# Holding one pass of table writes at TensorE's steps, as the loop around it does

## The chip, the cores and the metric

The kernel runs on one core of a Trainium2 chip. The metric is the device time of one execution in microseconds, lower being better. The kernel before takes 1842.63 us, the median of three runs (1838.82 to 1842.83).

## The reference

Two transformer layers over 32 batches (`B`) of 256 tokens with 256 features. The first layer is cross attention with relu instead of softmax, followed by a feed-forward network with weights of plus and minus one. The second is a cross attention with one memory row per query picked by argmax, and then a mixture of 64 experts, of which each token uses 8, with 128 places for each expert. Cut to what matters here:

```python
x = x + tanh(g_xattn[0]) * L0_xattn(layernorm(x), ctx, ctx)
x = x + tanh(g_ffn[0])   * L0_ffn(layernorm(x))
x = x + tanh(g_xattn[1]) * L1_xattn(layernorm(x), ctx)
h = layernorm(x).reshape(-1, H)                 # 8192 tokens
shared = silu(gu[:, :Is]) * gu[:, Is:] @ shared_down_w * sigmoid(h @ shared_gate_w)
w, idx = top_k(softmax(h @ gate_w), 8)
pos = running count of tokens per expert        # over all tokens, in order
buf[e_flat, min(pos, 128)] = h[tok]             # rows handed to the experts
y = sum over 8 of out_e[e_flat, slot] * w       # 0 where pos >= 128
x = x + tanh(g_ffn[1]) * (y + shared)
```

## The kernel before

Each engine has its own program, written out by hand; the engines meet only through semaphores. The work on a batch is cut into four stages, and the stages of four batches overlap: in pass `n`, TensorE computes the feed-forward network of batch `n` (`b_l0`, `b_l1`, `b_l2`), the first attention of batch `n+1`, the second attention and the shared expert of batch `n-1` (`c_...`, `d_gu`), and the end of batch `n-2` (`d_dn`, `d_cp`). The hand-written sequences `first(n)` and `second(n)` set TensorE's order.

Passes -1 to 2 stand outside a hardware loop, passes 3 to 30 are the loop (`Fori(3, NB - 1)`, with `NB` 32), and pass 31 stands outside again. Then come `first(32)` and `last_batch(31)`, called the drain below, and the 64 experts.

For every batch, GpSimd (POOL) writes 128 token rows at a time to a table in memory, sorted by expert: `scatter(b, group)`, an indirect DMA at L637 that moves 128 rows of 321 numbers. A batch needs 16 of these, cut in eleven groups `a` to `k` (2, 1, 1, 2, 1, 1, 1, 1, 2, 2 and 2 writes). POOL's pass `n` issues groups `g` to `k` of batch `n-3` and `a` to `f` of batch `n-2`, between its other duties. These are `take_ctx` (a copy), `take_keys` (operands of the next attention logits), `keep_x1` (a copy at L648), and `ln_coef`, the inverse root of the layer norms at L653, for which VectorE (DVE), then ScalarE (ACT) and then TensorE wait.

In the loop, seven of the eleven groups (`a`, `b`, `f`, `g`, `h`, `j`, `k`) are held: POOL waits for a step of TensorE and then runs a tiny filler operation (`plain`, L579, pool_pad) before it issues the write. The steps are the transposition of the attention's output (`tr_rdy[4]`, L1240) for `a` and `b`, the third part of the shared expert (`gu_rdy`, L1031) for `f`, the first two pairs of `b_l0` (`l0_rdy`, L1117) for `g` and `h`, the first attention logits (`lg_rdy`, L1193) for `j`, and the first transposition of the probabilities (`pt_rdy`, L1208) for `k`. In the code outside the loop the condition `not isinstance(b, int)` leaves all this out, and a group goes out as soon as POOL comes to it.

The order of POOL's pass 31 is: `g` and `h` of batch 28, `take_ctx`, `i`, `j`, `k` of batch 28, `take_keys`, `a` and `b` of batch 29, `keep_x1`, `ln_coef(3, 30)`, `c` and `d`, `ln_coef(2, 31)`, `e` and `f`. Behind the pass follow `g` to `k` of batch 29 and the batches 30 and 31. On SyncE, `pass_rows(29)` (L418) overwrites the rows in SBUF after the 16 writes of batch 28 have landed, and loads of expert weights are queued behind it.

Of the kernel before, what the change touches and what calls it, by code (L numbers as in the profile page):

```python
# [18 lines left out]
NB, S, D = 32, 256, 256  # L19
# [74 lines left out]
def build(nc, x, ctxT, maskT, g_xattn, g_ffn, wq0, wk0, wv0, bq0, bk0, bv0, k0, k1, k2, s0, s1, s2,  # L94
          wqT1, wkvT1, wcT1, gates_w, sgu_w, sdown_w, e_wts, out, table):
    es = ExitStack()
    with es:
# [249 lines left out]
        def written(b):  # L347

            return (xs_z, slot_z) if isinstance(b, int) and b == NB - 1 else (xs, slot)
# [177 lines left out]
        def _(pool):  # L527
# [49 lines left out]
            def plain(site):  # L577

                return g.tensor_tensor(pool_pad[:, site:site + 1], pad_in[:, :], pad_in[:, :], ALU.mult)  # L579
# [41 lines left out]
            def scatter(b, group):  # L621
                if group == "a":
                    pool.wait_ge(slots_ok, b + 1)
                    pool.wait_ge(tok_ok, b + 1)
                    pool.wait_ge(xr_out, 16 * b + 16)
                paced = {"a": (tr_rdy[4], b + 2), "b": (tr_rdy[4], b + 2), "f": (gu_rdy.sem, gu_rdy.nth(2, b + 1)), "g": (l0_rdy.sem, l0_rdy.nth(0, b + 3)),
                         "h": (l0_rdy.sem, l0_rdy.nth(1, b + 3)), "j": (lg_rdy.sem, lg_rdy.nth(0, b + 2)),
                         "k": (pt_rdy.sem, pt_rdy.nth(0, b + 2))}
                if not isinstance(b, int):
                    if group in paced:  # L630
                        pool.wait_ge(*paced[group])
                    if group in paced:
                        plain(8 + "abcdefghijk".index(group))
                rows, slots = written(b)
                for i in GROUPS[group]:
                    t, k = divmod(i, TOPK)
                    g.indirect_dma_start(  # L637
                        out=table, out_offset=bass.IndirectOffsetOnAxis(ap=slots[:, t, k:k + 1], axis=0),
                        in_=rows[:, t, :], in_offset=None, bounds_check=NT - 1, oob_is_err=False,
                    ).then_inc(scattered, 16)  # L640
# [40 lines left out]
            def body(n):  # L681
                m, c, d, e = n + 1, n - 1, n - 2, n - 3
                if on(e):
                    scatter(e, 'g')
                    scatter(e, 'h')
                if on(n):
                    take_ctx(n)
                if on(e):
                    scatter(e, 'i')
                    scatter(e, 'j')  # L690
# [1337 lines left out]
```

## Time and profile before

| what | value |
| --- | --- |
| median of three runs | 1842.63 us |
| lowest and highest run | 1838.82, 1842.83 us |
| profiled execution | 1847.19 us |
| its span, first to last instruction | 1845.2 us |
| PE, DVE, POOL, ACT busy | 91%, 72%, 55%, 52% of the span |
| one pass of the loop | 47.4 us |
| pass 31, outside the loop | 57.3 us |
| the drain, to the first expert | 83 us |
| TensorE's mean granted clock | 0.969 |

The profile is one execution on the chip. PE is TensorE. A pass is bounded here by the start of the last part of `d_gu` in two successive passes. A row of a timeline gives start and duration of an instruction, and in brackets how long its engine had been idle before it and what ended that; "issue" and "remote" mean that nothing the profile shows ended it. In the table, pass 31 does the same work as a pass of the loop less the first stage of a next batch.

### The profile page before, as it was taken

Reading aid. Unit: us, or ns where it says so; the run is one execution under the profiler, and the core shown is the slowest. Engines: PE = TensorE matmul, PEld = TensorE weight load, DVE = VectorE, ACT = ScalarE, POOL = GpSimd, SP = SyncE. Lnnn points to the kernel's source line nnn. Section 1 sums busy time; section 2 is a strip of 40 time slices with the busy share of each in tenths; the row PEclk is TensorE's granted clock in tenths of the full one; section 3 lists DMA queues with packets and bytes.
Section 4 is the critical chain, followed back from the end, with each engine's and each line's share of the span. In section 5 each row is a group of like instructions: output and inputs, shape, how many; then the busy total and the mean of one; then the engine's idle time right before and its main releaser. Section 6 shows DMA issues by size and latency. Waiting matters only on the chain.

```text
span 1845.2 us, 51326 instructions
## 1 busy us (share of the span) xinstructions
PE 1681.7 (91%) x17188; PEld 1418.1 (77%) x17188; DVE 1330.1 (72%) x4610; ACT 964.5 (52%) x2789; POOL 1023.1 (55%) x1627
## 2 busy tenths in 40 slices
PE   5799999999999999999999999999999998458785
PEld 4588888888788888878888888888888876347775
DVE  5477777777677777777777787777777865436554
ACT  3455555555555555555555555555555544214443
POOL 4125666666566666655666666666666653345555
PEclk9899999999999999999999999999999998579999
DMA  7411111111111111101111111111010012138886
GB/s 235 141 17 48 50 46 44 47 51 39 30 30 28 37 26 43 29 21 30 33 30 26 33 26 26 26 27 26 25 30 21 21 57 74 48 96 215 197 198 136
DMA packets 134336, 108.98 MB, mean 59 GB/s; under 512 B 70559, under 2 KB 123753, under 8 KB 134296
## 3 DMA queue, kind: packets, MB, share of 16 engines
q1 hardware_dynamic: 100504, 89.30, 16.7%
q0 software_dynamic: 33792, 19.17, 5.9%
q8 instruction: 22, 0.36, 0.1%
q14 instruction: 18, 0.15, 0.0%
HBM read 51.63 MB, written 111.84 MB: 89 GB/s over the span
## 4 chain that ended last, share of the span: by engine, by line
PE 69%; DMA 8%; DVE 7%; issue 6%; ACT 4%; another core or an unknown queue 4%; POOL 2%; SPq 0%; POOLq 0%; DVEq 0%; ACTq 0%
PE bank L1133 22%; PE bank L1031 8%; DMA out<-ey,aid 6%; PE bank L1117 6%; PE ps_yo L1031 4%; PE ps_m L1031 4%; PE ps_lg L1193 4%; PE ps_lg L1031 3%; PE ps_yo L1149 3%; PE ps_tr L1057 3%; PE ps_m L1231 2%; PE ps_pt L1031 2%; PE ps_pt L1208 2%; ACT xr L774 2%
## 5 line engine op out<-in xcount | busy, mean ns | idle before, releaser
L637 POOL DMA_INDIRECT table<-xs,slot x496 | 505.4, 1019 | 199.3 <-issue 171.8
L1133 PE MATMUL bank<-h_h,held 128*128 128x256 f16 x2048 | 267.6, 274 | 2.8 <-DVE h_l L1616 1.7
L1133 PE MATMUL bank<-h_l,held 128*128 128x256 f16 x2048 | 266.9, 273 | 0.7 <-issue 0.7
L579 POOL TENSOR_TENSOR pool_pad<-pad_in 128x1 f32<-128x1 f32 x382 | 75.0, 196 | 325.4 <-PE ps_tr L1240 163.8
L838 ACT ACTIVATE p<-ps_lg,rmax 128x77 f32<-128x77 f32 x1024 | 235.5, 351 | 7.3 <-DVE rmax L1681 7.0
L1133 PEld LDWEIGHTS bank<-h_l,held 128*128 128x128 f16 x2048 | 201.2, 98 | 25.0 <-issue 1.1
L1133 PEld LDWEIGHTS bank<-h_h,held 128*128 128x128 f16 x2048 | 193.7, 98 | 25.4 <-issue 3.3
L1616 DVE SCALAR_TENSOR_TENSOR h_l<-bank,h_h 128x512 f16<-128x512 f32 x256 | 175.0, 684 | 27.8 <-ACT h_h L824 22.4
L653 POOL TENSOR_TENSOR rs<-nt,minushalf 128x2 f32<-128x2 f32 x128 | 92.5, 722 | 163.5 <-DVE nt L1578 152.4
L844 ACT ACTIVATE pt_h<-ps_pt 128x384 f16<-128x384 f32 x128 | 62.8, 491 | 189.0 <-PE ps_pt L1208 189.0
L741 POOL DMA_INDIRECT out<-ey,aid x64 | 98.7, 1542 | 97.1 <-DVE aid L1963 57.4
L1681 DVE TENSOR_REDUCE rmax<-ps_lg 128x8 f32<-128x616 f32 x128 | 102.1, 797 | 54.6 <-PE ps_lg L1193 52.1
L824 ACT ACTIVATE h_h<-bank 128x512 f16<-128x512 f32 x128 | 76.6, 598 | 119.1 <-PE bank L1133 119.1
L819 ACT ACTIVATE h_h<-bank 128x512 f16<-128x512 f32 x128 | 76.4, 597 | 92.4 <-PE bank L1117 92.4
L1149 PE MATMUL ps_yo<-held,h_h 128*128 128x256 f16 x512 | 118.2, 276 | 0.1
L1149 PE MATMUL ps_yo<-held,h_l 128*128 128x256 f16 x512 | 118.0, 273 | 0.0
L1117 PE MATMUL bank<-xt_h,held 128*128 128x256 f16 x512 | 99.5, 277 | 8.3 <-DVE dn_l L1510 5.9
L1565 DVE BATCH_NORM_STATS2 stats<-x 128x6 f32<-128x256 f32 x256 | 96.0, 417 | 13.4 <-DMA x<-in_x 3.7
L1031 PE MATMUL bank<-xt_h,gu_h 128*128 128x256 f16 x512 | 99.3, 276 | 0.8 <-DVE ac L1770 0.6
L1031 PE MATMUL bank<-xt_l,gu_h 128*128 128x256 f16 x512 | 99.4, 276 | 0.0
L1117 PE MATMUL bank<-xt_l,held 128*128 128x256 f16 x512 | 99.3, 276 | 0.0
L1031 PE MATMUL bank<-xt_h,gu_l 128*128 128x256 f16 x512 | 99.2, 276 | 0.0
(279 smaller groups left out, 4574.9 us busy)
## 6 DMA issues: line engine op xcount, KB each, us to landing
ew<-in_e_wts SPq DMA_DIRECT2D x48, 384.0 KB
table<-xg SPq DMA_DIRECT2D x8, 1284.0 KB, 15.9
xg<-table SPq DMA_DIRECT2D x64, 160.5 KB
xs<-xr SPq DMA_DIRECT2D x31, 320.0 KB, 2.7
x<-in_x SPq DMA_DIRECT2D x32, 256.0 KB
out<-x SPq DMA_DIRECT2D x32, 256.0 KB
table<-xs,slot POOLq DMA_INDIRECT x496
held<-in_e_wts SPq DMA_DIRECT2D x16, 384.0 KB, 4.4
```

What stands on the lines that cost most here:

```text
L637: g.indirect_dma_start(out=table, out_offset=bass.IndirectOffsetOnAxis(ap=slots[:, t, k:k + 1], axis=0), in_=rows[:, t, :], in_offset=None ...
L653: g.tensor_tensor(rs[i][:, :], nt[i][:, 0, :], minushalf[:, :], ALU.pow).then_inc(ln_root[i], 1)
L741: g.indirect_dma_start(out=out, out_offset=bass.IndirectOffsetOnAxis(ap=aid[u][:, 0:1], axis=0), in_=ey[u][:, :], in_offset=None, bounds_c ...
L824: a.activation(h1_h[:, 2 * j:2 * j + 2, :], two(bank[j % 2]), ACT.Relu).then_inc(l1_hi.sem, 1)
L838: ins = a.activation(p32[:, h * S2:(h + 1) * S2], ps_lg[:, h // HB, h % HB * S2:(h % HB + 1) * S2], ACT.Exp, bias=rmax[r % 2][:, h:h + 1])
L1031: ins = mm(out_, s_, m_, start=(start and i == 0), stop=(stop and i == len(seq) - 1))
L1117: ins = mm(two(bank[j % 2])[:, m % 2, :], s_, m_, start=(k == 0), stop=(k == 3))
L1133: ins = mm(two(bank[j % 2])[:, m % 2, :], wb1[:, k, m * P:(m + 1) * P], hp[:, k, :], start=(i == 0 and k == 0), stop=(i == 1 and k == FK - 1))
L1149: ins = mm(two(ps_yo)[:, t, :], hp[:, k, t * P:(t + 1) * P], wb2[:, k, :], start=(i == 0 and k == 0), stop=(i == 1 and k == FK - 1))
L1565: last = v.bn_stats(stats[i][:, t, :], src[:, t, :])
L1616: v.scalar_tensor_tensor(hl[:, 2 * j:2 * j + 2, :], two(bank[j % 2]), 0.0, hh[:, 2 * j:2 * j + 2, :], ALU.max, ALU.subtract).then_inc(lo.s ...
L1681: v.tensor_reduce(rmax[r % 2][:, :].rearrange("p (g h) -> p g h", g=2), lg, AX, ALU.max, negate=True).then_inc(z_ok.sem, 1)
```

## The change

One condition in `scatter` is widened. Batch 28 (`NB - 4`, groups `g` to `k`) and groups `a` to `f` of batch 29 (`NB - 3`) are now held too, wherever they stand outside the loop, which is pass 31. The waits and the fillers are those of the loop, seven of each.

```diff
@@ scatter(b, group) @@
-                if not isinstance(b, int):
+                if not isinstance(b, int) or b == NB - 4 or b == NB - 3 and group in "abcdef":
                     if group in paced:
                         pool.wait_ge(*paced[group])
                     if group in paced:
                         plain(8 + "abcdefghijk".index(group))
```

No other engine's program changes, nor does POOL's before pass 31. POOL's first row after the loop's branch was two writes (`g`, `h`); each now has its wait for `l0_rdy` ahead of it.

POOL in the middle of pass 31, behind `take_ctx` and up to the filler of `take_keys`. The rows L637 are table writes (groups `i`, `j`, `k` of batch 28), the rows L579 fillers with the semaphores they wait for:

```order
-L637 DMA table<-xs,slot 8192x321 x6
+L637 DMA table<-xs,slot 8192x321 x2
+L579 TENSOR_TENSOR pool_pad<-pad_in 128x1 [waits lg_rdy]
+L637 DMA table<-xs,slot 8192x321 x2
+L579 TENSOR_TENSOR pool_pad<-pad_in 128x1 [waits pt_rdy]
+L637 DMA table<-xs,slot 8192x321 x2
 L579 TENSOR_TENSOR pool_pad<-pad_in 128x1 [waits lg_rdy,vc_ok,vp_ev,kp_ev]
```

Six writes in a row became three pairs, of which the second waits for the logits and the third for the transposed probabilities of batch 30.

POOL behind `take_keys` in the same pass. The writes are groups `a` and `b` of batch 29, L648 is the copy of `keep_x1`, L653 the root of `ln_coef(3, 30)`:

```order
-L637 DMA table<-xs,slot 8192x321 [waits xr_out,tok_ok,slots_ok]
-L637 DMA table<-xs,slot 8192x321 x2
+L579 TENSOR_TENSOR pool_pad<-pad_in 128x1 [waits xr_out,tr_rdy4,tok_ok,slots_ok]
+L637 DMA table<-xs,slot 8192x321 x2
+L579 TENSOR_TENSOR pool_pad<-pad_in 128x1 [waits tr_rdy4]
+L637 DMA table<-xs,slot 8192x321
 L648 COPY x_kept<-x 128x512 [waits x2_ok,x1_ok]
 L653 TENSOR_TENSOR rs<-nt,minushalf 128x2 [waits ln_st3]
```

The three writes, and so the copy and the root behind them, now wait for the transposed attention output of batch 30.

POOL at the end of the pass, where `e` and `f` of batch 29 are followed at once by its `g` to `k`:

```order
 L653 TENSOR_TENSOR rs<-nt,minushalf 128x2 [waits ln_st2]
-L637 DMA table<-xs,slot 8192x321 x10
+L637 DMA table<-xs,slot 8192x321
+L579 TENSOR_TENSOR pool_pad<-pad_in 128x1 [waits gu_rdy]
+L637 DMA table<-xs,slot 8192x321 x9
```

Nine of the ten writes now stand behind a wait for the third part of the shared expert.

## Rows read from the trace of the kernel before

**Rows 1.** The first line of the page.

```profile
span 1845.2 us, 51326 instructions
```

**Rows 2.** Stretches: span; PE, PEld, DVE, ACT, POOL busy; clock; DMA share, GB/s.

```profile
1457.20:1504.70 47.50, 45.37 (x492) 37.98 (x489) 35.88 (x126) 25.41 (x77) 28.05 (x49) 1.00 0.18 55
1504.70:1562.00 57.30, 49.47 (x477) 39.16 (x477) 34.83 (x116) 24.98 (x74) 23.28 (x32) 0.91 0.18 60
```

**Rows 3.** Line L848 on ACT in the whole trace: count, durations, what ended its idle.

```profile
L848 ACT ACTIVATE vb<-ps_tr x32: 511/511/512, 80.8 to 1575.7; 128x408 f16<-128x408 f32 x32
...
  PE ps_tr L1215: 67.9, 31
  remote: 6.9, 1
```

**Rows 4.** Timelines of ACT, DVE and PE in pass 31: start, duration, instruction.

```profile
1521.26 0.51 ACT L848 ACTIVATE vb<-ps_tr 128x408 f16<-128x408 f32 x1 [6.92 <-remote]
...
1518.37 0.80 DVE L1681 TENSOR_REDUCE rmax<-ps_lg 128x8 f32<-128x616 f32 x1 [2.04 <-remote]
...
1515.72 0.47 PE L1215 MATMUL ps_tr<-vc,wide 77*128 77x34 f16 x12
...
1518.34 0.60 PE L1133 MATMUL bank<-h_h,held 128*128 128x256 f16 x4 [0.29 <-issue]
...
1521.20 0.93 PE L1133 MATMUL bank<-h_l,held 128*128 128x256 f16 x7 [0.45 <-issue]
```

**Rows 5.** Timeline of POOL, from the last loop pass into the drain.

```profile
1488.12 0.20 POOL L579 TENSOR_TENSOR pool_pad<-pad_in 128x1 f32<-128x1 f32 x1 [5.79 <-PE ps_tr L1240]
...
1500.29 1.04 POOL L637 DMA_INDIRECT table<-xs,slot  x1 [2.75 <-issue]
...
1511.68 0.19 POOL L579 TENSOR_TENSOR pool_pad<-pad_in 128x1 f32<-128x1 f32 x1 [3.06 <-PE ps_tr L1031]
...
1512.54 1.01 POOL L637 DMA_INDIRECT table<-xs,slot  x1 [0.16 <-issue]
...
1518.99 0.98 POOL L637 DMA_INDIRECT table<-xs,slot  x1 [0.30 <-issue]
1535.93 0.19 POOL L579 TENSOR_TENSOR pool_pad<-pad_in 128x1 f32<-128x1 f32 x1 [15.96 <-PE ps_lg L1193]
...
1544.10 0.63 POOL L648 COPY x_kept<-x 128x512 f32<-128x512 f32 x1
1550.21 0.72 POOL L653 TENSOR_TENSOR rs<-nt,minushalf 128x2 f32<-128x2 f32 x1 [5.49 <-DVE nt L1578]
...
1569.62 0.97 POOL L637 DMA_INDIRECT table<-xs,slot  x1 [0.30 <-issue]
1594.54 0.97 POOL L637 DMA_INDIRECT table<-xs,slot  x1 [23.95 <-DVE slot L1761]
```

**Rows 6.** Timeline of PE, the steps for which the held groups would wait.

```profile
1515.49 0.29 PE L1193 MATMUL ps_lg<-kb_h,qp_l 64*128 64x308 f16 x2
...
1525.17 0.90 PE L1208 MATMUL ps_pt<-ident,p 128*128 128x128 f32 x3
...
1542.57 0.76 PE L1240 MATMUL ps_tr<-ident,att 128*128 128x128 f32 x4 [0.72 <-DVE att L1694]
...
1558.75 0.38 PE L1031 MATMUL bank<-xt_h,gu_l 128*128 128x256 f16 x2
```

**Rows 7.** Stretches in which TensorE was granted half of its clock.

```profile
1522.50:1529.30 6.80, 5.27 (x28) 3.63 (x29) 4.74 (x20) 4.50 (x18) 0.00 (x0) 0.50 0.15 52
1542.90:1546.30 3.40, 3.40 (x18) 2.44 (x17) 1.29 (x2) 1.08 (x2) 1.59 (x2) 0.51 0.04 5
```

**Rows 8.** Timelines of DVE and SyncE: who waits for the copy; a late step; the row copy.

```profile
1554.65 0.75 DVE L1630 SCALAR_TENSOR_TENSOR x<-ps_yo,sc,x_kept 128x512 f32<-128x512 f32 x1 [0.54 <-PE ps_yo L1149]
...
1569.34 0.24 DVE L1643 MAX8 am<-ps_tr 128x8 f32<-128x77 f32 x1 [4.04 <-issue]
...
1527.82 0.60 SPq L418 DMA_DIRECT2D xs<-xr  x1
```

## The prediction, made before the changed kernel ran

> **What bounds the kernel now.** I read the stretches first, since the change touches one pass of 32. The last pass of the loop takes 47.50 us, and pass 31 takes 57.30 us for no more work [rows 2]: DVE, ACT and POOL are all less busy in it, and TensorE's granted clock is 0.91 instead of 1.00. So pass 31 holds 9.8 us over a pass of the loop, and that is all the change can get at, in a span of 1845.2 us [rows 1]. About 1.9 us of it comes from before the change's reach: POOL issued group `d` of batch 29 after an idle of 2.75 us with no cause in the profile [rows 5], still inside the loop's last pass, and the last part of `d_gu` behind it is that much late. This leaves 7.9 us.
>
> Next I looked at where those 7.9 us arise, by engine. ACT's copy at L848 waits for TensorE's L1215. In 31 of its 32 executions its idle ended with that step (67.9 us in all, 2.2 us each); once it was 6.92 us with nothing to end it [rows 3]. That once is pass 31: L1215 was over at 1515.72 + 0.47 = 1516.19, and ACT began at 1521.26 [rows 4], 5.1 us late. All softmax steps of batch 30 are queued behind it on ACT. In the same microseconds DVE had an idle of 2.04 us without a cause, ended at 1518.37, and TensorE, in a run of matmuls that wait for nobody, went in pieces from 1518.34 to 1521.20 [rows 4]. Three engines halt together, and the one thing that goes on is POOL's table writes: six, from 1512.54 to 1518.99 + 0.98 = 1519.97, one each 1.29 us [rows 5]. The passes 1 and 2 stand outside the loop as well, and their L848 is among the 31 without a halt. So straight-line code alone doesn't make it; straight-line code together with a dense stream of writes is what this place has to itself. A second such halt stands in the drain: DVE's L1643 with 4.04 us of idle without a cause at 1569.34 [rows 8], again inside a stream, whose last write starts at 1569.62 [rows 5].
>
> After the halt the clock goes down: TensorE has half of it (1.2 of 2.4 GHz) from 1522.5 to 1529.3 and from 1542.9 to 1546.3 [rows 7]. These two stretches hold 5.27 and 3.40 us of PE work, which at the upper level would be half of that, so up to 2.6 + 1.7 = 4.3 us hang on it.
>
> **The change part by part.** Seven fillers of 0.2 us and their waits on POOL: 1.4 us of work, and an estimated 0.9 us from the end of the step waited for to the write. POOL has 15.96 us of idle before `take_keys` and 5.49 us before the root at 1550.21 [rows 5], so nothing of that is paid as such. What matters is when each piece comes out.
>
> `g` and `h`: their steps, two pairs of the first layer, lie before the step of TensorE on which the filler at 1511.68 waits [rows 5]. They go out before it, and `take_ctx` and `i` (1512.54) stay where they are. Cost nothing.
>
> `j`: its step, the logits, ends at 1515.49 + 0.29 = 1515.78 [rows 6]. The writes come at about 1516.6 and 1517.9, 1.5 us later than before (third and fourth place in the stream, 1515.1 and 1516.4).
>
> `k`: its step begins at 1525.17 [rows 6] and comes from ACT's softmax, behind the halt. The two writes leave the stream (they were at 1517.7 and 1518.99) and come at about 1526.9 and 1528.2. POOL is done by 1529.2, 6.7 us before `take_keys` at 1535.93, less what that step comes earlier. SyncE's copy of the rows, at 1527.82 now [rows 8], must wait for their landing and comes about 2.5 us later, as do the weight loads queued behind it on SyncE. Nobody on this pass waits for them before `a` does, and `a` is held past that. Cost nothing.
>
> So instead of six writes between 1512.5 and 1520.0 there are four, and the last is out at 1518.9. What does the halt give back? From below: ACT began 1.29 us after the last write was out; with the last write 1.1 us earlier it begins 1.1 us earlier. From above inside this reading: the halt goes with the number of writes, and 5.1 us times 2/6 is 1.7 us. I take 1.5 us. The clock stays low in the same stretches, since three and a half microseconds of halt remain.
>
> `a` and `b`: the step ends at 1542.57 + 0.76 = 1543.33 [rows 6]. Writes from 1544.2, three of them with a second filler until about 1548.3, then the copy, which ends at about 1549.0 instead of 1544.73. DVE wants the copy at 1554.65 [rows 8], 5.6 us later. The root behind it started at 1550.21, on DVE's word [rows 5]: slack 1.2 us. Cost nothing while that holds.
>
> `f`: the third part of the shared expert ends near 1559.1 (its last matmuls start at 1558.75 [rows 6]), the write comes 0.8 us later than before, and so do the nine behind it. The stream ends at 1571.4 instead of 1570.6. POOL's next write had to wait until 1594.54 anyway [rows 5]. But the DVE halt at 1569.34 lies in this stream and could stretch with it: 0 to 0.8 us. I take 0, since it ended before the stream did.
>
> Sum: -1.5 + 0 = -1.5 us, with ends -0.3 (1.1 given back, 0.8 paid) and -1.7. The profiled execution would take 1847.19 - 1.5 = 1845.7 us. It lies 4.6 us over the median of the three runs, so I carry the difference over to the median: 1842.63 - 1.5 = 1841.1, say 1841 us.
>
> The Trainium skill bears on why the engines halt. Its page Runtime: NRT & Kernel Launch, section Instruction fetch mechanics, says that an engine's code is fetched by DMA in blocks while the block before runs, and that this is mostly hidden. By that page alone, thinning out the writes would give 0 us; the halt of 5.1 us [rows 4] is not hidden here. Its page DMA: Bandwidth & Descriptors, section Queues, rings and completion order, says that a DMA engine takes turns between queues packet by packet, by which a fetch would be slowed by every write in flight. No row read here shows a fetch waiting.
>
> **The rivals.** *The halt goes away whole.* With never more than two writes back to back, as in the passes of the loop, the three engines may never halt. For it speaks that 31 of 32 executions of L848 have none [rows 3]; against it, that `i` and `j` still put four writes in 6.4 us where the halt begins. It gives back 5.1 us, and up to 4.3 us of clock [rows 7], but no more than the 7.9 us left over: 1842.6 - 7.9 = 1834.7 us.
>
> *The halt has nothing to do with the writes.* All engines leave the loop here within some microseconds, and the halt may belong to that. DVE's and ACT's halts both start within 12 us of the pass's beginning at 1504.7; POOL's idle of 2.75 us [rows 5] came with no stream at all, which speaks for this. Then POOL's writes move in idle time and the time is 1842.6 us.
>
> *Slower: the hold uses up POOL's cover ahead of the root.* Before, POOL sat idle for 5.49 us ahead of the root at 1550.21. Now it has 1.2 us. If POOL has a halt of its own between 1543 and 1550, the root of `ln_coef(3, 30)` is late, and DVE, ACT and TensorE's next transposition with it, on the path. It decides from 1.2 us on. A halt of POOL's known size, 2.75 us, costs 1.5 us; one of ACT's 5.1 us costs 3.9, and with the clock held down as in the second stretch [rows 7] 5.6 us. Its middle is +3: 1845.6 us. POOL's code has grown by seven fillers and their waits, so that a halt may fall elsewhere than before.
>
> **How the numbers follow.** The forecast has 0.36, the whole halt gone 0.26, no connection 0.24, slower 0.14. The lower end of the range is 1834, just under the first rival; the upper is 1845, which leaves out about half of the slower case and, below, some of the first rival where the runs scatter down by their 4 us: together under 0.2. A measurement of this kernel can tell about 0.3%, 5.5 us, from no change. Only the first rival goes past it downward: 0.26. Upward goes the far end of the slower case, and a little for what I have not thought of: 0.06. The rest, 0.68, is within.
>
> **What would show it.** In the changed trace, pass 31 between the same two steps takes 55.8 us by the forecast, 49.4 if the halt is gone, 57.3 without a connection. ACT's L848 has its one long idle shortened to about 5.4 us by the forecast, to 2.2 if the halt is gone. `k` is issued after the first transposition at L1208, the copy L648 comes at about 5 us after the filler for L1240, and the root after it must still be ended by DVE's nt; if it starts straight after the copy, the slower case holds. The half-clock stretch after 1522 stays in the forecast and goes in the first rival. The forecast is wrong if the halt keeps its length while the last write moves forward, or if a halt of the same kind turns up at a place that had none, on POOL above all.

## The result, and the profile after

The changed kernel took 1835.42 us (median of 13 runs, 1830.50 to 1837.67), the kernel before on the same chip 1841.92 us (13 runs, 1838.75 to 1847.60). The ratio is 0.9958, with a 95% interval of [0.9947, 0.9968], so 0.4% faster; between the medians lie 6.5 us. The time lies in the range of the prediction and near its first rival, not near the forecast of 1841. As will be seen, the figure holds for one sort of chip only. The ratios here and below are taken over all runs of both kernels and needn't equal the ratio of the two medians.

The profiled execution of the changed kernel took 1833.93 us. Its page begins, against [rows 1]:

```profile
span 1832.2 us, 51334 instructions
```

Eight instructions more: seven fillers, and one wait that has an instruction of its own. The two stretches that answer to [rows 2] (span; PE, PEld, DVE, ACT, POOL busy; clock; DMA share; GB/s):

```profile
1454.58:1502.00 47.42, 45.25 (x491) 37.84 (x489) 35.88 (x126) 25.40 (x76) 28.05 (x48) 1.00 0.19 55
1502.00:1551.35 49.35, 45.72 (x471) 37.63 (x472) 34.89 (x116) 24.97 (x74) 23.96 (x38) 0.97 0.21 70
```

The last pass of the loop is as it was. Pass 31 went from 57.30 to 49.35 us, so 7.95 us came back, and the clock in it rose from 0.91 to 0.97. Of the 13.0 us between the two spans, another 2.7 us arose before pass 31 begins (1502.0 for 1504.7), where the change does nothing; a second profile of the changed kernel, below, doesn't have them. 3.0 us came from the drain and 0.65 us went back in the experts. One execution against one can be off by some microseconds: the profiled one of the kernel before took 1847.19 us, 5.3 us over the median of its 13 runs, and the medians say 6.5. There is no second profile of the kernel before, on either sort of chip.

ACT's L848, against [rows 3], over the whole trace:

```profile
L848 ACT ACTIVATE vb<-ps_tr x32: 511/511/511, 81.4 to 1563.3; 128x408 f16<-128x408 f32 x32
...
  PE ps_tr L1215: 68.1, 32
```

All 32 now end their idle with TensorE's step; the long one with "remote" is gone. The timelines of the place, against [rows 4] and [rows 6], first ACT, then DVE, then PE:

```profile
1512.83 0.51 ACT L848 ACTIVATE vb<-ps_tr 128x408 f16<-128x408 f32 x1 [1.88 <-PE ps_tr L1215]
...
1513.04 0.80 DVE L1681 TENSOR_REDUCE rmax<-ps_lg 128x8 f32<-128x616 f32 x1
...
1512.33 0.47 PE L1215 MATMUL ps_tr<-vc,wide 77*128 77x34 f16 x12
1512.78 1.03 PE L1133 MATMUL bank<-h_h,held 128*128 128x256 f16 x8
...
1516.37 0.31 PE L1193 MATMUL ps_lg<-mrow,row 64*128 64x308 bf16 x2
...
1516.99 0.55 PE L1208 MATMUL ps_pt<-ident,p 128*128 128x128 f32 x3
```

From L1215 to L848's start there were 5.54 us before (1515.72 to 1521.26) and there are 0.50 now (1512.33 to 1512.83). DVE doesn't wait at L1681, and TensorE's matmuls at L1133 stand in whole groups of eight. L1208 comes 4.66 us after L1215, where it came 9.45 us after it, and runs at the full clock (0.55 us instead of 0.90).

POOL, against [rows 5]:

```profile
1509.53 1.01 POOL L637 DMA_INDIRECT table<-xs,slot  x1 [0.16 <-issue]
...
1512.57 0.19 POOL L579 TENSOR_TENSOR pool_pad<-pad_in 128x1 f32<-128x1 f32 x1 [0.74 <-PE ps_lg L1193]
...
1514.61 0.98 POOL L637 DMA_INDIRECT table<-xs,slot  x1 [0.30 <-issue]
1517.63 0.19 POOL L579 TENSOR_TENSOR pool_pad<-pad_in 128x1 f32<-128x1 f32 x1 [2.04 <-PE ps_pt L1208]
1518.35 1.00 POOL L637 DMA_INDIRECT table<-xs,slot  x1 [0.53 <-issue]
...
1533.21 0.20 POOL L579 TENSOR_TENSOR pool_pad<-pad_in 128x1 f32<-128x1 f32 x1 [5.08 <-PE ps_tr L1240]
...
1537.67 0.63 POOL L648 COPY x_kept<-x 128x512 f32<-128x512 f32 x1
1540.05 0.72 POOL L653 TENSOR_TENSOR rs<-nt,minushalf 128x2 f32<-128x2 f32 x1 [1.75 <-DVE nt L1578]
...
1549.03 0.18 POOL L579 TENSOR_TENSOR pool_pad<-pad_in 128x1 f32<-128x1 f32 x1 [0.39 <-PE bank L1031]
...
1560.30 0.99 POOL L637 DMA_INDIRECT table<-xs,slot  x1 [0.30 <-issue]
```

`i` and `j` are four writes between 1509.53 and 1515.59, `k` stands alone behind L1208, the root is still ended by DVE. The last write of the stream behind `f` starts at 1560.30. DVE in that stream, against [rows 8]:

```profile
1555.62 0.24 DVE L1643 MAX8 am<-ps_tr 128x8 f32<-128x77 f32 x1 [1.11 <-issue]
...
1561.42 0.48 DVE L1659 TENSOR_SCALAR mrow<-ps_tr 128x308 bf16<-128x308 f32 x1 [3.98 <-remote]
```

The idle ahead of L1643 shrank from 4.04 to 1.11 us, and one of 3.98 us turned up further on, ahead of L1659, where the kernel before had 1.24 us, ended by TensorE's L1176. For [rows 7], the same places of pass 31 (17.8 and 38.2 us after its start) hold no lowered clock:

```profile
1519.80:1526.60 6.80, 6.80 (x93) 5.41 (x91) 4.62 (x11) 3.90 (x16) 1.60 (x5) 1.00 0.53 176
1540.20:1543.60 3.40, 3.09 (x25) 2.12 (x24) 1.11 (x3) 1.69 (x3) 2.60 (x3) 1.00 0.01 0
```

One stretch of 3.4 us at half the clock remains in the pass, from 1533.5 to 1536.9.

**What a halt is.** "remote" and "issue" say only that the profile found no one to blame, since TensorE's row had long ended. The trace also records when each semaphore was written, and that settles who was waited for. In the kernel before, the semaphore that L1215 raises was written at 1521.24, 5.06 us after the end of the row (1516.19 by the profile); ACT's row starts 0.02 us later. The one that L1193 raises was written at 1518.35, 2.56 us late, and DVE's L1681 starts at 1518.37. So the waiting engines weren't halted at all: they waited for TensorE's completions, and those were late. TensorE's own rows go with it: in the pieces of [rows 4] they start again at 1518.34 and at 1521.20, within 0.04 us of the two writes. From the same records, for the steps whose reader began right then:

| step of TensorE | written after the row's end, before | with the change |
|---|---|---|
| L1193, pass 31 | 2.56 us | 0.02 us |
| L1215, pass 31 | 5.06 us | 0.01 us |
| L1031 (`qp`), drain | 3.68 us | 0.74 us |
| L1176, drain | 0.77 us | 3.62 us |
| L1031 (`gw`), drain | 2.58 us | 1.84 us |
| L1031 (`ps_yo`, read by L1780), drain | 2.71 us | 0.41 us |
| L1231, median of the first of each loop pass | 1.70 us | 1.72 us |
| most others in the loop, median | 0.01 us | 0.01 us |

The Trainium skill, Perfetto Trace Analysis, section Per-instruction lifecycle: what the profiler-reported window actually captures, says that TensorE's end time is an estimate from the size of the instruction, while its semaphore is pushed when PSUM has acknowledged the bytes. The trace agrees that the row's end is no measurement: the two are 0.01 us apart as a rule and 5.06 us apart once. It doesn't show what happened in the 5.06 us.

### The profile page after: what moved, and what is told of

It reads as the page before. It is cut to its first block, busy times and chain, and to the rows that moved or that the text cites. A ratio compares the mean times of both kernels' runs of the same rounds, so it can differ in the third digit from the quotient of the medians.

```text
span 1832.2 us, 51334 instructions
## 1 busy us (share of the span) xinstructions
PE 1670.9 (91%) x17188; PEld 1413.6 (77%) x17188; DVE 1331.1 (73%) x4610; ACT 964.8 (53%) x2789; POOL 1027.4 (56%) x1634
## 4 chain that ended last, share of the span: by engine, by line
PE 68%; DMA 8%; DVE 7%; issue 6%; ACT 4%; another core or an unknown queue 4%; POOL 3%; SPq 0%; POOLq 0%; DVEq 0%; ACTq 0%
PE bank L1133 22%; PE bank L1031 8%; DMA out<-ey,aid 6%; PE bank L1117 6%; PE ps_yo L1031 4%; PE ps_m L1031 4%; PE ps_lg L1193 4%; PE ps_lg L1031 3%; PE ps_yo L1149 3%; PE ps_tr L1057 2%; PE ps_m L1231 2%; POOL table L637 2%; PE ps_pt L1031 2%; PE ps_pt L1208 2%
## 5 line engine op out<-in xcount | busy, mean ns | idle before, releaser
L637 POOL DMA_INDIRECT table<-xs,slot x496 | 507.4, 1023 | 194.1 <-issue 192.8
L1133 PE MATMUL bank<-h_h,held 128*128 128x256 f16 x2048 | 265.8, 273 | 1.7 <-DVE h_l L1616 1.7
L1133 PE MATMUL bank<-h_l,held 128*128 128x256 f16 x2048 | 266.3, 273 | 0.0
L579 POOL TENSOR_TENSOR pool_pad<-pad_in 128x1 f32<-128x1 f32 x389 | 75.9, 195 | 320.2 <-PE ps_tr L1240 169.1
L1133 PEld LDWEIGHTS bank<-h_l,held 128*128 128x128 f16 x2048 | 200.8, 98 | 23.6
L1133 PEld LDWEIGHTS bank<-h_h,held 128*128 128x128 f16 x2048 | 192.9, 98 | 23.4 <-issue 1.8
L653 POOL TENSOR_TENSOR rs<-nt,minushalf 128x2 f32<-128x2 f32 x128 | 93.0, 727 | 157.2 <-DVE nt L1578 145.3
L1681 DVE TENSOR_REDUCE rmax<-ps_lg 128x8 f32<-128x616 f32 x128 | 102.1, 798 | 48.3 <-PE ps_lg L1193 47.8
L1031 PE MATMUL bank<-xt_h,gu_h 128*128 128x256 f16 x512 | 98.4, 274 | 1.7 <-DVE ac L1770 1.6
L1031 PE MATMUL bank<-xt_h,gu_l 128*128 128x256 f16 x512 | 98.5, 274 | 0.0
L1031 PE MATMUL bank<-xt_l,gu_h 128*128 128x256 f16 x512 | 98.4, 274 | 0.0
```

What stands on the lines that cost most here:

```text
L637: g.indirect_dma_start(out=table, out_offset=bass.IndirectOffsetOnAxis(ap=slots[:, t, k:k + 1], axis=0), in_=rows[:, t, :], in_offset=None ...
L653: g.tensor_tensor(rs[i][:, :], nt[i][:, 0, :], minushalf[:, :], ALU.pow).then_inc(ln_root[i], 1)
L1031: ins = mm(out_, s_, m_, start=(start and i == 0), stop=(stop and i == len(seq) - 1))
L1133: ins = mm(two(bank[j % 2])[:, m % 2, :], wb1[:, k, m * P:(m + 1) * P], hp[:, k, :], start=(i == 0 and k == 0), stop=(i == 1 and k == FK - 1))
L1681: v.tensor_reduce(rmax[r % 2][:, :].rearrange("p (g h) -> p g h", g=2), lg, AX, ALU.max, negate=True).then_inc(z_ok.sem, 1)
```

## The experiments

The chips on which runs were made fall in two sorts, which I call A and B. The kernel before took 1841.92 and 1839.72 us in the two sessions on sort A (whether on one chip or two isn't recorded), and 1790.56, 1790.88, 1791.27 and 1794.37 us on sort B, three chips, one of them used twice. Which chip a run lands on can't be chosen. Of the kernels with an edit only the changed one came to both sorts; all those with a part of the change met sort B. That limits what follows.

**The change once more.** No edit; the kernel of the result.

> The change itself, measured again. In the four runs before this one the kernel before took 1790.6 us instead of 1841.9, ACT's L848 had no long idle even where the six writes stood in one stream, and DVE's first L1692 of a pass had lost the idle of 2.1 us without a cause that it has in 29 of 32 passes of the first traces. Theory D (the halts belong to the chip or to where the program lies on it): if the kernel before takes about 1790 us here too, the ratio is 0.999 to 1.002; if it takes about 1842 us, the ratio is 0.995 to 0.997. Theory A alone (dense writes halt the engines everywhere) would have given 0.996 in either case, and is already against the four runs.

On a chip of sort A: 1833.67 us (1830.60 to 1836.94) against 1839.72 us, ratio 0.9973, [0.9959, 0.9987]. Its stretch from L1215 of pass 31 to L1215 of the drain, and DVE in the drain:

```profile
1515.12:1566.79 51.67, 41.01 (x427) 33.05 (x426) 30.44 (x110) 20.45 (x64) 25.38 (x34) 0.96 0.20 66
...
1565.42 0.48 DVE L1659 TENSOR_SCALAR mrow<-ps_tr 128x308 bf16<-128x308 f32 x1 [5.33 <-remote]
```

The same stretch in the trace of the kernel before, and in the first trace of the changed one:

```profile
1515.72:1575.15 59.43, 45.90 (x427) 35.05 (x426) 30.78 (x111) 20.50 (x64) 23.63 (x29) 0.87 0.17 57
```

```profile
1512.33:1562.76 50.43, 41.10 (x427) 33.15 (x426) 30.70 (x109) 20.56 (x64) 25.37 (x34) 0.97 0.20 68
```

So 7.8 us come back in this stretch in the second profile and 9.0 in the first. In the second it begins at 1515.12, where the kernel before had 1515.72: the 2.7 us ahead of pass 31 were not the change's. The late completion at L1215 is gone in both profiles, the one ahead of L1659 is new in both.

**The change a third time.** No edit.

> The changed kernel once more. So far the kernel before took 1840 to 1842 us on two chips and 1790 to 1791 us on two others; the change was timed only on the former (ratios 0.9958 and 0.9973). Theory A: the gain is the halt of pass 31, and the halt exists only where a loop pass takes 47.4 us and TensorE's completions come late. Then here: if the kernel before takes about 1840 us, the ratio is again 0.995 to 0.998; if it takes about 1791 us, the ratio is 0.999 to 1.002, with pass 31 as long with the change as without. Rival B: the order of the writes has a worth of its own (TensorE's order suits the work behind it). Then the ratio is 0.996 to 0.998 on either kind of chip.

On a chip of sort B: 1797.43 us (1789.82 to 1799.32) against 1794.37 us (1790.85 to 1797.89), ratio 1.0013, [0.9998, 1.0027]. The stretches from L1215 to L1215, of pass 30 and of pass 31:

```profile
1427.24:1475.50 48.26, 46.69 (x507) 39.43 (x506) 38.14 (x130) 27.05 (x80) 28.97 (x49) 1.00 0.18 55
1475.50:1521.92 46.42, 40.96 (x428) 33.09 (x426) 30.87 (x111) 20.52 (x64) 23.38 (x32) 0.96 0.22 73
```

Theory A gets its number (0.999 to 1.002), rival B doesn't (0.996 to 0.998): the order of the writes has no such worth of its own there. In these runs the change gave something only where completions are late. The kernel before has no profile on sort B; the trace of "batch 29 alone" below, which leaves batch 28 as it was, takes 46.11 us between the same two steps (1477.08 to 1523.19), so 46.42 is not shorter.

**Half of the change at a time.** Batch 28 alone, batch 29 alone, and fillers without waits:

```
-                if not isinstance(b, int):
+                if not isinstance(b, int) or b == NB - 4:                          # batch 28 alone
+                if not isinstance(b, int) or b == NB - 3 and group in "abcdef":    # batch 29 alone
```

```
-                if not isinstance(b, int):
-                    if group in paced:
-                        pool.wait_ge(*paced[group])
+                if not isinstance(b, int) and group in paced:
+                    pool.wait_ge(*paced[group])
+                if not isinstance(b, int) or b == NB - 4 or b == NB - 3 and group in "abcdef":
```

> Only batch 28 is held (g, h, j, k), that is the writes up to take_keys; a, b and f of batch 29 go as before. Theory A: the whole gain in pass 31, ratio about 0.996 to 0.9965, L848 without a long idle. Theory C (the gain comes from the later copy and root behind a and b): none of it, ratio 1.0.

> Only a, b and f of batch 29 are held; the six writes of batch 28 stand in one stream as before. Theory A: L848 keeps its long idle, ratio 0.999 to 1.001. Theory C: the gain of the change, 0.996.

> The seven fillers stand in pass 31 as in the change, but none of the waits. POOL's code is as long as in the change and the writes go out as early as before, 0.2 to 0.5 us further apart. Theory A (the engines halt because table writes stream densely while they run code that is executed once): the six writes behind take_ctx still stand in one stream, ACT's copy L848 keeps its one long idle of about 7 us, and the time is that of before within 0.2% (0.998 to 1.002). Theory B (the gain comes from POOL's code being longer, which moves where a halt falls): the gain of the change, ratio about 0.996, L848 without the long idle.

All on one chip of sort B, where the kernel before took 1790.56 us (35 runs): batch 28 alone 1792.96 us, ratio 1.0017, [1.0008, 1.0026]; batch 29 alone 1791.00 us, 1.0003, [0.9994, 1.0013]; fillers alone 1791.61 us, 1.0008, [0.9997, 1.0019]. Fillers alone again on a second chip of that sort:

> Fillers without waits again, since the first four runs fell on a chip without the halts (kernel before 1790.6 us). Told by the kernel before in the same call. At about 1840 us: theory A (dense writes and code that is executed once, together) expects ACT's L848 with its long idle of about 7 us and a ratio of 0.999 to 1.001; theory B (POOL's code is longer, and a halt falls elsewhere) 0.996 to 0.998 and no long idle. At about 1790 us: ratio 1.000 and no long idle by both.

1791.50 us against 1790.88, ratio 1.0007, [0.9994, 1.0020]. None of them tells which half gives the gain, because there was no halt to remove; that there was none is what they show. "Batch 29 alone" leaves batch 28 as in the kernel before, with its six writes in a row while TensorE is at L1193 and L1215; POOL and ACT's L848 in its trace:

```profile
1473.90 1.01 POOL L637 DMA_INDIRECT table<-xs,slot  x1 [0.16 <-issue]
...
1480.36 0.98 POOL L637 DMA_INDIRECT table<-xs,slot  x1 [0.30 <-issue]
...
L848 ACT ACTIVATE vb<-ps_tr x32: 510/510/511, 80.5 to 1523.7; 128x408 f16<-128x408 f32 x32
...
  PE ps_tr L1215: 64.1, 32
```

Six writes from 1473.90 to 1481.34, L1215 at 1477.09 in the middle of them, and ACT waits at L848 as in any other pass. On sort B, then, the stream by itself delays no completion; on sort A no run tested it alone.

**Only `j` and `k`.** The two groups that fill the second half of that stream are held, nothing else.

```
-                if not isinstance(b, int):
+                if not isinstance(b, int) or b == NB - 4 and group in "jk":
```

> Only j and k of batch 28 are held, g and h go as early as before. Theory A in its narrow form (what counts is the stream of six behind take_ctx): the gain of the change, 0.996, L848 without a long idle. If g and h matter too (eight writes in 14 us instead of six in 7.5), part of the idle stays: 0.997 to 0.999.

> Only j and k of batch 28 held, again. With the kernel before at about 1840 us theory A expects the gain of the change, 0.996 to 0.998, and no long idle ahead of L848; if the hold of g and h is what counts, the idle of about 7 us stays and the ratio is 1.000. At about 1790 us: ratio 1.000.

> Only j and k of batch 28 held. Two calls gave a kernel before of 1790.6 and 1790.9 us without any halt, one call and the first measurement about 1840 us with halts. If this one has the kernel before at about 1840 us: theory A (the stream of six writes behind take_ctx meets code that is executed once) expects the gain of the change, 0.996 to 0.998, and no long idle ahead of ACT's L848; if g and h or a, b and f matter, the idle of about 7 us stays or the ratio is 0.999 to 1.001. At about 1790 us: 1.000 to 1.002.

> Only groups j and k of the pass of batch 28 wait for their steps; all else is as before. Theory A (what ends the halt is that the two writes of k leave the stream of six): where the kernel before takes about 1840 us, pass 31 loses its late completion at L1215 and the ratio is 0.995 to 0.998; where it takes about 1791 us, 1.000 to 1.002, as the earlier three. Rival C (the gain comes from the hold of a, b and f in batch 29, or from nothing in the order but from the place of the code): 0.999 to 1.001 where the kernel before takes about 1840 us, with the step at L1215 still about 5 us late.

Sort B each time: 1791.29 us, ratio 1.0007 [0.9997, 1.0018]; 1794.44 us, 1.0014 [0.9998, 1.0029]; 1795.87 us, 1.0009 [0.9990, 1.0029]; 1796.88 us, 1.0010 [0.9996, 1.0024]. For the cause of the halt they are inconclusive. For sort B they say something: these four, batch 28 alone (1.0017) and the whole change (1.0013) all lie about 0.1% above one, 1 to 3 us by the ratios. Only one interval leaves one out, and the fillers without waits, at 1.0008 and 1.0007, lie there as well, so this can't be put down to the waits. I found no stretch that holds the difference: the time from L1215 of the drain to the end of the span goes from 262 to 273 us among the profiles of sort B, more than what is looked for.

**The stream of six, moved.** `i`, `j` and `k` of batch 28 stay six writes in a row, but the row is held until the first L1208, behind the place of the halt.

```
-                if not isinstance(b, int):
-                    if group in paced:
-                        pool.wait_ge(*paced[group])
-                    if group in paced:
-                        plain(8 + "abcdefghijk".index(group))
+                if not isinstance(b, int) and group in paced:
+                    pool.wait_ge(*paced[group])
+                    plain(8 + "abcdefghijk".index(group))
+                elif isinstance(b, int) and b == NB - 4 and group == "i":
+                    pool.wait_ge(*paced["k"]); plain(18)
```

> The six writes of i, j, k stay one stream, but the stream starts only after TensorE's first L1208, some 5 to 10 us later than before. One filler, no other hold. With the kernel before at about 1840 us: if what counts is where the stream stands against the moment at which ACT, DVE and PE cross into code not yet read (about 11 us after the pass begins), L848 has no long idle and the ratio is 0.996 to 0.998; if a dense stream halts whoever runs, a halt of 3 to 5 us turns up at another step, at L1681, L844 or L838, and the ratio is 0.999 to 1.001. At about 1790 us: ratio 1.000, no halt.

> The six writes of i, j and k of batch 28 stay one stream, but the stream is held until TensorE's first L1208; a, b and f of batch 29 are not held. Theory A1 (a stream of six writes makes whichever completion of TensorE falls behind it come late): where the kernel before takes about 1840 us, the halt moves behind the first L1208 and stays some 5 us, ratio 0.999 to 1.001. Rival A2 (the halt hangs on writes at that one place, before L1215 of the pass, not on the number): the halt goes, ratio 0.995 to 0.998. Where the kernel before takes about 1791 us both say 1.000, as the earlier run.

Sort B again: 1791.25 us against 1790.88, ratio 0.9999 [0.9987, 1.0012], and 1793.39 us against 1794.37, ratio 0.9992 [0.9981, 1.0004]. POOL in the second:

```profile
1484.90 0.19 POOL L579 TENSOR_TENSOR pool_pad<-pad_in 128x1 f32<-128x1 f32 x1 [8.50 <-PE ps_pt L1208]
1485.64 1.02 POOL L637 DMA_INDIRECT table<-xs,slot  x1 [0.54 <-issue]
...
1492.08 0.97 POOL L637 DMA_INDIRECT table<-xs,slot  x1 [0.30 <-issue]
```

No late completion behind it either. Whether on sort A the halt would have followed the stream (A1) or stayed away (A2) stays open.

The pair also measures what the lowered clock costs. The same kernel, from L1215 of pass 31 to L1215 of the drain, once with and once without such a stretch, on two chips of sort B:

```profile
1476.97:1523.19 46.22, 40.68 (x428) 33.19 (x426) 30.63 (x111) 20.44 (x64) 25.21 (x31) 0.96 0.22 74
```

```profile
1479.75:1524.44 44.69, 39.16 (x427) 32.19 (x426) 30.62 (x111) 20.40 (x64) 25.18 (x31) 1.00 0.23 76
```

The first had half the clock for 3.4 us, from 1496.6 to 1500.0, and is 1.53 us longer, near what half the clock takes from 3.4 us of matmuls, 1.7 us; two profiles of the kernel with only `j` and `k` held give 46.37 at 0.96 and 44.70 at 1.00, so 1.67 us.

## Why the prediction came out as it did

**What bounds the kernel.** Right: the gain is in pass 31, 7.95 us, against the 7.9 us that were called the most that could be had, and POOL's 2.75 us of idle ahead of it stayed outside the change's reach.

**The step that failed** is the size of the one term that counted: "the halt goes with the number of writes, and 5.1 us times 2/6 is 1.7 us. I take 1.5 us." L1215's lateness went from 5.06 to 0.01 us, not to 3.4. The term measured 7.95 us: 5.0 us for the halt, and nearly 3 us with it, of which the vanished stretch at half the clock explains 2.6 (half of its 5.27 us of matmuls [rows 7]). That is the first rival's sum: pass 31 took 49.35 us where that rival said 49.4, the forecast 55.8 and "no connection" 57.3, and the 6.8 us at half the clock behind the halt went with it, as only this rival had it. The time was 1835.4 us where it said 1834.7. It had a chance of 0.26. That the time lies within the range is luck as far as the mechanism goes: the lower end had been put just under this rival. The rival's clock term was too large itself, 4.3 us with both stretches of [rows 7], and came out only because the sum was capped at 7.9 us: the stretch of 3.4 us wasn't the halt's. It stays with the change (1533.5 to 1536.9), and one like it stands in nine of the eleven profiles of sort B.

Two things could have been read better. Behind the number stood the picture of three engines held up by a thing in proportion to the writes. The semaphores' record was in the trace of the kernel before, and it says that one engine, TensorE, was late and two waited for it. And the row that spoke for the forecast over the rival, that `i` and `j` still put four writes in 6.4 us where the halt begins, came true, with 6.06 us, and the completion came in time all the same.

**The other terms.** `g`, `h`: nothing, as costed. `j`: its first write was forecast 0.8 us after the end of L1193's last matmuls and came 0.9 us after it (1513.30 against 1512.39). `k`: forecast 1.7 us behind the start of L1208, came 1.36 us behind it (1518.35); SyncE's row copy now starts at

```profile
1521.82 0.60 SPq L418 DMA_DIRECT2D xs<-xr  x1
```

which is 4.83 us behind L1208's start instead of 2.65, so 2.2 us later where 2.5 were forecast, and nobody waited for it. `a`, `b`: the copy L648 comes 4.46 us behind the filler, forecast about 5. `f`: its cover was said to be 23.95 us of POOL's idle behind the stream, and 19.89 us of it are left, so nothing was paid.

**The slower rival** did not come. The root kept 1.75 us of slack where 1.2 were forecast, and POOL had no halt between the copy and the root. On sort B the whole change measured 1.0013, with one inside the interval and 1.0027 as its end, so a cost of 3 us is not excluded there, but not by that mechanism: in that trace DVE's nt ended the root's wait too, after 1.76 us of idle. POOL's 2.75 us of idle, which the prediction counted for the second rival and as the size of a halt that might come, is another thing than the late completions: it stands at the same place, 2.75 or 2.76 us long, in all 14 profiles, on sort B as well.

**What the forecast did not hold at all:** 3.0 us from the drain. The clock was lower before. From the end of pass 31 to the first load for the experts, before and with the change:

```profile
1562.00:1645.33 83.33, 36.56 (x288) 24.68 (x285) 31.75 (x128) 17.84 (x61) 38.78 (x40) 0.63 0.17 53
```

```profile
1551.35:1631.68 80.33, 32.19 (x290) 22.64 (x290) 31.74 (x128) 17.75 (x61) 40.32 (x41) 0.71 0.17 55
```

At 0.63 of the clock TensorE was busy for 36.56 us, at 0.71 for 32.19, with the same matmuls. Cut at two steps that stand on the chain of work that ended last, in both traces, the drain shows where the time went:

| stretch of the drain | length, PE busy, clock before | with the change |
|---|---|---|
| start to L1215 | 13.15, 6.97 us, 0.81 | 11.41, 5.71 us, 1.00 |
| to DVE's L1692 at 1590.95 (1577.29) | 15.80, 9.28 us, 0.50 | 14.53, 8.01 us, 0.65 |
| to the first load for the experts | 54.38 us | 54.39 us |

All 3.0 us arise ahead of that L1692, and TensorE's busy time there fell by 2.5 us. The late steps ahead of L1215 cancel (3.68 us and 0.77 before, 0.74 and 3.62 with the change). Those behind L1692 are 0.7 us (L1031 `gw`) and 2.3 us (L1031 `ps_yo`) less late and gave nothing: the load follows the start of POOL's last table write by 2.08 and 2.09 us, and these writes run on for over 10 us behind the reader of `ps_yo`. So the clock is the likely cause of the 3.0 us; no run here holds it fixed. In the second profile the rest of the span behind L1215 of the drain took 268.4 us, against 270.1 before and 269.4 in the first.

**And the second rival?** "The halt has nothing to do with the writes" is right on sort B, where there is none. On sort A it is wrong in its result. Its argument isn't refuted: that the stretch from L1215 to L1215 gives back 7.8 to 9.0 us there is shown in two profiles, that the writes of `k` are what made L1215 late is not. The new late step, L1176 ahead of L1659, stands in a stream of nine writes; the kernel before had ten there, with that step only 0.77 us late. This fits a reading in which some completions are late at places that move when anything is shifted; the kernel with `k` alone held or the stream moved would tell it apart on such a chip, and never met one.

**What speaks against one candidate.** The reading of code was a candidate, since 16 KB blocks of it are fetched in pass 31. DMA queues of the kernel before (packets, MB, share of 16 engines), from 1512.0 to 1513.5, ahead of the halt:

```profile
q8 instruction: 1, 0.02, 4.5%
```

4.5% of sixteen engines over 1.5 us is one packet of 1.08 us. In the whole run there are 22 of them, and 22 with the change, on sort A and sort B alike, from 0.88 to 1.7 us each; within the loop there are none, and yet one completion in each pass of it is late on sort A. A second queue of that kind moves 8 KB packets; one of them, of 0.31 us, stands at 1515.6, and has its like in the same place on sort B (1475.1, L1215 at 1475.5), where nothing is late. TensorE's rows also kept their pace for 2 us behind L1215 while its completion was out, one group of eight each 0.87 us:

```profile
1516.03 1.03 PE L1133 MATMUL bank<-h_h,held 128*128 128x256 f16 x8
1516.90 1.04 PE L1133 MATMUL bank<-h_l,held 128*128 128x256 f16 x8
1517.78 0.27 PE L1133 MATMUL bank<-h_h,held 128*128 128x256 f16 x1
```

So a slow fetch is an unlikely cause. The Trainium skill, Runtime: NRT & Kernel Launch, section Instruction fetch mechanics, has the code fetched in 16 KiB blocks while the current one runs, at a cost that is mostly hidden. The packets of the first queue agree with it in size; on sort B no completion is late behind one, and no run here shows a fetch that was waited for.

## What to carry to other kernels

Where an engine waits with "remote" or "issue" and the step it needs had long ended by the profile, compare the time at which the step's semaphore was written before forming a theory: here it came 5 us after the end of TensorE's row. Before costing such a wait, look at its pattern over the whole kernel (once, or once in each pass), and don't scale it with what happens to run beside it. And a gain of 0.4% that hangs on a wait without a cause has to be measured on more than one chip: here it was 0.42 and 0.27% on one sort and nothing on the other.

## What the runs showed of the hardware

**Chips differ by 2.5 to 2.9% on the same program.** The kernel before takes 1840 to 1842 us on one sort and 1791 to 1794 us on the other, at the same granted clock over the run (0.969 to 0.976 in the profiles of sort A, 0.972 to 0.976 in those of sort B). Most of it is in the loop: from L1215 to L1215 a pass takes 47.44 us on one sort and 46.27 us on the other, 1.17 us for each of 28, and L1215 of pass 31 comes 31 to 40 us earlier. The one step that is late in each pass of the loop on sort A, and in none on sort B, is the last L1231 ahead of DVE's first L1692; that it makes up the 1.17 us is likely, but no run shows it. DVE's L1692 in the kernel before (sort A), then in the changed kernel on sort B:

```profile
L1692 DVE RECIPROCAL rden<-ps_m x128: 197/208/209, 91.2 to 1597.3; 128x8 f32<-128x8 f32 x128
...
  remote: 62.7, 29
  PE ps_m L1231: 11.4, 37
```

```profile
L1692 DVE RECIPROCAL rden<-ps_m x128: 197/208/208, 90.5 to 1542.3; 128x8 f32<-128x8 f32 x128
...
  PE ps_m L1231: 24.9, 65
```

And the place in one pass, TensorE and DVE, on sort A and on sort B:

```profile
1476.34 0.18 PE L1231 MATMUL ps_m<-vb,pt_l 128*128 128x34 f16 x1
1476.36 1.03 PE L1133 MATMUL bank<-h_h,held 128*128 128x256 f16 x8
...
1478.24 0.21 DVE L1692 RECIPROCAL rden<-ps_m 128x8 f32<-128x8 f32 x1 [2.13 <-remote]
```

```profile
1437.80 0.18 PE L1231 MATMUL ps_m<-vb,pt_l 128*128 128x34 f16 x1
1437.83 1.03 PE L1133 MATMUL bank<-h_h,held 128*128 128x256 f16 x8
...
1438.02 0.21 DVE L1692 RECIPROCAL rden<-ps_m 128x8 f32<-128x8 f32 x1 [0.44 <-PE ps_m L1231]
```

The same matmuls start at the same pace, and the completion arrives 1.7 us late on one chip and at once on the other. In none of the eleven profiles of sort B is a completion of TensorE with a reader waiting, over 1100 in each, more than 0.03 us late; in the three of sort A 40 to 48 are more than 0.6 us late. What makes them late on sort A is not known from these runs.
